# All 36 edge lookups of a pair in one block on TensorE, with three steps moved on VectorE

## The reference

```python
# graph layer, on layernorm(x)
ft = (feat @ W).reshape(n, H, OUT)                 # 4 heads of 64
e = e_src[src] + e_dst[dst]                        # per edge and head
e = where(e >= 0, e, 0.2 * e)
ex = exp(e - segment_max(e, dst)[dst])
a = ex / segment_sum(ex, dst)[dst] * dist
x = x + segment_sum(ft[src] * a, dst)
# experts, on layernorm(x): all eight for every node, weighted by a softmax over the experts
h = relu(bn1(x @ W1[e] + b1[e])); h = relu(bn2(h @ W2[e] + b2[e])); y = h @ Wo[e] + bo[e]
x = x + sum_e w[f, e] * y[f, e]
```

## Time and profile before

| | us |
|---|---|
| median of 3 runs | 1619.68 |
| lowest and highest | 1618.13, 1620.72 |
| the profiled execution | 1621.68 |
| its span, first to last instruction | 1620.1 |

### The profile page before, as it was taken

One profiled execution on the slowest core, in us unless ns is written; L12 is line 12 of the kernel. 1 busy time (PEld: TensorE's weight loads), 2 busy tenths in 40 slices (PEclk: granted clock), 3 DMA queues, 4 the chain that ended last, 5 costly groups with the idle time before them and its releaser, 6 DMA issues.

```text
span 1620.1 us, 23895 instructions
## 1 busy us (share of the span) xinstructions
PE 1492.8 (92%) x8358; PEld 1298.6 (80%) x8358; DVE 1184.3 (73%) x2195; ACT 749.2 (46%) x1341; POOL 1015.4 (63%) x934
## 2 busy tenths in 40 slices
PE   3670689999999999999999999999999999999998
PEld 2450577878888888888888888888888888888887
DVE  4660654578877887888788788878877887888751
ACT  1340133245555545545545555555455555545553
POOL 1027657767777777777777777777777777777000
PEclk9885799999999999999999999999999999999999
DMA  7765434434344434443443444343344434343000
GB/s 189 218 194 149 128 93 120 125 112 117 108 125 117 127 104 131 110 125 110 115 125 106 126 116 131 100 129 113 109 126 115 128 103 128 111 128 89 10 3 11
DMA packets 106161, 187.49 MB, mean 116 GB/s; under 512 B 38479, under 2 KB 70596, under 8 KB 106011
## 3 DMA queue, kind: packets, MB, share of 16 engines
q0 software_dynamic: 44144, 123.00, 27.6%
q1 hardware_dynamic: 61337, 62.42, 13.3%
q10 hardware_dynamic: 560, 0.52, 0.2%
HBM read 172.72 MB, written 14.42 MB: 116 GB/s over the span
## 4 chain that ended last, share of the span: by engine, by line
PE 70%; DVE 11%; issue 7%; ACT 4%; DMA 3%; SPq 3%; POOL 2%; ACTq 0%; DVEq 0%
PE bankH L786 35%; PE bankY L815 17%; PE bankE L745 5%; PE bankE L746 5%; PE bankE L738 3%; DMA table<-gath 3%; ACT msg_hi L967 3%; POOL gath L637 2%; DVE onehot L1345 2%; SPq L386 2%; PE bankB L723 1%; DVE x L1459 1%; DVE stats L1408 1%; DVE x L1406 1%; DVE x L1402 1%
## 5 line engine op out<-in xcount | busy, mean ns | idle before, releaser
L637 POOL DMA_INDIRECT gath<-table,src_win x900 | 1003.5, 1115 | 399.3 <-issue 224.6
L995 ACT ACTIVATE h<-bankH,bn_shift,bn_scale 128x250 f32<-128x250 f32 x800 | 401.7, 553 | 482.9 <-PE bankH L786 478.0
L786 PE MATMUL bankH<-h,w 128*128 128x250 f32 x1600 | 448.1, 399 | 0.0
L786 PE MATMUL bankH<-xT,w 128*128 128x250 f32 x1600 | 378.5, 379 | 1.6 <-ACT xT L981 1.4
L815 PE MATMUL bankY<-wo,h 128*125 128x256 f32 x1600 | 378.1, 379 | 1.1 <-DVE x L1459 1.1
L815 PEld LDWEIGHTS bankY<-wo,h 128*125 128x125 f32 x1600 | 296.2, 188 | 42.4 <-issue 1.4
L786 PEld LDWEIGHTS bankH<-xT,w 128*128 128x128 f32 x1600 | 296.9, 192 | 33.7 <-ACT xT L981 1.1
L1390 DVE TENSOR_TENSOR msg_lo<-gath,msg_hi 128x2340 fp32r<-128x2340 f32 x88 | 228.4, 2595 | 95.7 <-ACT msg_hi L967 95.7
L786 PEld LDWEIGHTS bankH<-h,w 128*128 128x128 f32 x1600 | 279.6, 199 | 18.1
L1459 DVE SCALAR_TENSOR_TENSOR x<-bankY,gate,x 125x256 f32<-125x256 f32 x400 | 174.0, 476 | 154.0 <-PE bankY L815 153.8
L967 ACT ACTIVATE msg_hi<-gath 128x2340 fp32r<-128x2340 f32 x88 | 189.2, 2150 | 190.7 <-PE bankE L746 190.7
(11 more groups left out here) (181 smaller groups left out, 972.9 us busy)
## 6 DMA issues: line engine op xcount, KB each, us to landing
onehot_t<-dst_low SPq DMA_DIRECT2D x48, 576.0 KB, 5.2
gath<-table,src_win POOLq DMA_INDIRECT x900, 2.8
x_res<-in_x SPq DMA_DIRECT2D x25, 250.0 KB
out<-x SPq DMA_DIRECT2D x25, 250.0 KB
table<-gath SPq DMA_DIRECT2D x25, 227.5 KB
w<-in_L_ffn_W SPq DMA_DIRECT2D x8, 512.0 KB, 5.5
wo<-in_L_ffn_Wo SPq DMA_DIRECT2D x4, 512.0 KB, 6.1
gath<-in_x SPq DMA_DIRECT2D x1, 2016.0 KB
```

What stands on the lines that cost most here:

```text
L637: pool.indirect_dma_start(gath[:, g.slot(u), t, :], None, table, bass.IndirectOffsetOnAxis(src_win[:, g.win, u, t:t + 1], 0)).then_inc(row ...
L786: mm = pe.matmul(target[:, hc * 2 * NT:(hc + 1) * 2 * NT], weights[:, e * KC + c, hc * P:(hc + 1) * P], operand(c), start=(c == 0), stop=( ...
L995: ins = act.activation(target[:, e % 2, hc, :, :].rearrange("p u n -> p (u n)"), source[:, hc * 2 * NT:(hc + 1) * 2 * NT], ACT.Relu, bias= ...
```

## The change

The 36 lookups of `a` are issued in one block, right behind `turn_bounds` in step `plan.bounds`; no `layer2` has lookups between its matmuls any more. On DVE, where `g` isn't late, `row_bounds(a)` goes from step 5 to the end of step 3, `runs(a)` comes ahead of `residual(g, 1)` in step 6, and `norm1(g, 0)` and `norm1(g, 1)` come behind that step's `add_y`. One row of the gathers is released in step 3 instead of step 4.

```diff
-BEHIND = (... (1, 1, 1, 2), (1, 2, 1, 2), ...)     # steps 3 and 4
+BEHIND = (... (1, 2, 1, 2), (1, 1, 1, 2), ...)
@@ PE, body
-                def between():
-                    for _ in range(2):
-                        next(small, None)
                     if a is not None and s == plan.bounds:
                         turn_bounds(f, a)
+                        for _ in small:
+                            pass
-                        layer2(*before(f, s, 1), between if 1 <= s <= 6 else nothing)
+                        layer2(*before(f, s, 1), nothing)
-                    if s == 6:
-                        for _ in small:
-                            pass
@@ DVE, body
-                    if a is not None and s == plan.bounds + 2:
+                    if a is not None and late(g) and s == plan.bounds + 2:
                         row_bounds(a)
                     ...
                             make_onehot(a, c)
+                    if a is not None and not late(a) and s == 6:
+                        runs(a)
                     if not late(g) and g is not None:
                         for u in plan.residuals.get(s, ()):
                             if u == 1:
                                 residual(g, u)
                     ...
-                    if a is not None and not late(a) and s == 6:
-                        runs(a)
-                    if f is not None and g is not None and not late(g) and s == max(plan.residuals):
-                        norm1(g, 0)
-                        norm1(g, 1)
                     if a is not None and not late(a) and s == 7:
                         edge_sum(a)
                         carries(a)
                     if run and (s >= 2 or not f.begins(1)):
                         add_y(*before(f, s, 2))
+                    if f is not None and g is not None and not late(g) and s == max(plan.residuals):
+                        norm1(g, 0)
+                        norm1(g, 1)
+                    if a is not None and not late(g) and s == plan.bounds:
+                        row_bounds(a)
```

More of the change, by code:

```diff
@@ L38 @@
 FROM = 5
-BEHIND = ((1, 1, 1, 0), (1, 1, 2, 0), (1, 1, 1, 2), (1, 1, 1, 2), (1, 2, 1, 2), (1, 1, 1, 2), (1, 1, 2, 0), (1, 1, 2, 0))
+BEHIND = ((1, 1, 1, 0), (1, 1, 2, 0), (1, 1, 1, 2), (1, 2, 1, 2), (1, 1, 1, 2), (1, 1, 1, 2), (1, 1, 2, 0), (1, 1, 2, 0))
 SEG = 2 * H
```

## The result

| | before | after |
|---|---|---|
| median of 20 runs each, us | 1620.57 | 1617.32 |
| lowest and highest | 1616.89, 1624.12 | 1613.13, 1619.19 |
| the profiled execution | 1621.68 | 1614.49 |
| its span | 1620.1 | 1612.9 |

The ratio is 0.9978, interval 0.9971 to 0.9985: the change makes the kernel faster by 0.22%, some 3.6 us. It was forecast to bring 9.1 us. The time is inside the range and the sign is right, but more than half of the forecast gain is missing.

A forecast was written before the change was run, and what follows sets the result against it. TensorE, busy 92% of the span, was taken to bound the kernel. Per steady body -1.04 + 1.76 - 0.33 - 0.33 - 0.49 = -0.43 us, -9.0 over 21, first two bodies -0.1: median 1610.6 us, range 1597 to 1619.

The forecast's parts named there:

- The price of the block: TensorE, step 3: 36 lookups in one group cost 2.28 us instead of 3.12 interleaved, saving 0.84 us a pair.
- The rival of lookups that are no cheaper: Block in step 3: each lookup costs 0.087 us, the block 3.12, body +0.41 us, kernel 1628; chance 6%.
- Steps 1 to 5: TensorE, steady body: steps 1 and 2 gain 1.04 us together, step 3 loses 1.76, steps 4 and 5 gain 0.33 each.
- Steps 6 and 7: Steady body: earlier start and no scans' wait, less a new `relu2` wait, bring 0.82 us, of which 0.49 is new.
- The wait for the scans: TensorE ahead of `turn_runs`, step 6: 0.61 us of waiting for VectorE's scans goes away with the reordering.
- The new wait for `relu2`: TensorE at `layer2` of expert 6, step 7: finds ScalarE's `relu2` unfinished and waits 0.65 us.
- the bodies of f = 0 and f = 1: First two full bodies: lookup savings -2.08 and -2.60 us, the block +2.28 in each, together -0.1 us.
- the fourth rival: TensorE's clock falls in the block: one layer a body at 1.2 GHz costs +1.68 us, kernel 1646; chance 2%.
- The sum: Whole kernel: -0.43 us per steady body, -9.0 over 21, first two bodies -0.1; median 1610.6 us.
- Without the `relu2` wait: Part of the rival that new waits don't come (18%): another 0.65 x 21 = 13.7 us saved, kernel 1597.
- Nothing holds TensorE inside the block for a one-hot: Answers the rival that release order makes TensorE wait inside the block for the second one-hot: 1619 us; chance 6%.
- The gathers are in time: Answers the rival that gathers come too late for `keep_esrc`: overrun by 0.4, the gain is gone, 1620 us; chance 8%.

The follow-up runs named there:

- r2_after: The changed kernel run once more with nothing altered, in a second set of runs: median 1615.84 us, ratio 0.9981 to the kernel before.
- e4_late_between: The changed kernel with the lookups of the bodies where `g` is late left between the matmuls of `layer2`: 1612.84 us, ratio 0.9958 to the kernel before.
- e5_relu2_late: `e4_late_between` with ScalarE's `relu2` of expert 5 ahead of both `root1` in step 6: 1600.96 us, ratio 0.9884 to the kernel before.
- e6_two_blocks: `e5_relu2_late` with the steady lookups in two blocks of 18, in steps 4 and 5: 1594.93 us, ratio 0.9850 to the kernel before.

## Why the prediction was right or wrong

- **The price of the block: right.** 2.21 us and 0.09 on the next layer (862.62 - 860.84 = 1.78 instead of 1.69), 2.30 in all; 2.28 was forecast. One lookup costs 0.061 us. The rival of lookups that are no cheaper (0.087) is out. The prediction's estimate by the Trainium skill, "TensorE: Matmul & The Clock Gate", section "Back-to-back issue gap", is out too: with its 81 ns a pair, given for 128 columns, 2.92 were to be expected, and for 12 columns this trace does not agree.
- **Steps 1 to 5: right.** -1.04 for steps 1 and 2 as forecast; +1.77 in step 3 (forecast +1.76); -0.36 each in steps 4 and 5 (forecast -0.33), where the loop from the chunk sum over `keep_high` and `low_part` takes 7.43 us (forecast 7.45).
- **Steps 6 and 7: the mechanism right, two sizes off.** Forecast -0.49, measured -0.34. The wait for the scans was taken as 2.14 - 1.53 = 0.61, the 1.53 from a `layer3` with a chunk sum behind it. With `turn_runs` behind it and no wait it takes 1.72, a case that the rows quoted did not hold. So only 0.42 of it was a wait; what follows a group changes the distance to the next start. The new wait for `relu2` was taken as 0.65 and is 0.57. The order of events was as forecast: 0.70 us of wait for `keep_esrc` (forecast 0.8), the scans, the second residual, `root1`, `relu2`. `norm1` behind `add_y` cost nothing, nor did `row_bounds` in step 3.
- **The step that failed: the bodies of f = 0 and f = 1, "together -0.1".** There the saving of each lookup was added up and the block's price set against it, with the price and the clock as in steady bodies. The medians say that they lose 3 to 4 us (the difference between the two groups of kernels). The traces say that it is two things: 2.7 us in the execution without a change of the clock, since savings ahead of a wait for VectorE only lengthen that wait and the block's own step costs more than in a steady body, and some 3 us more in the executions in which the clock falls behind the block. For the first, the forecast did not ask whether a saving in these bodies counts: TensorE waits there for the scans, 5.16 us at 215.06 in `r2_after` and 4.08 at 215.83 in `e4_late_between`, and that `turn_runs` starts 37.7 us behind the `turn_bounds` of the body before in both. For the second, the fourth rival, the clock falling in the block, was given 2% because the setup's block is at 1.00 after 2.07 us of idleness. In its form "one such layer a body" it is wrong. But the same row group that was quoted for it, an idle 3.85 us and a layer at half clock in the body of f = 1, said that just in these bodies the clock does fall.
- **The sum.** Terms as measured: 21 x -0.32 = -6.7 and +3.1 to +3.6 for the first bodies, against -9.0 and -0.1. The steady sizes explain 2.3 us of the miss, the first bodies 3.2 or more. That the time still fell inside the range says nothing for the term of the first bodies.
- **The other rivals.** Without the `relu2` wait the forecast gave 1597; that case is `e5_relu2_late`, and it took 1600.96, 3.96 over it. Its body is 0.90 us shorter than before, where -0.43 - 0.65 = -1.08 was forecast, and 21 x 0.18 = 3.8; the largest part is the 0.19 of the scans' wait that was none. Nothing holds TensorE inside the block for a one-hot: the next layer starts 2.20 us behind its start in the median of the steady bodies. The gathers are in time: L951 waits for them 4 times, the last time at 321.36 us, ahead of the steady bodies.
- **The whole block was worth less than its cover.** Of 0.84 us a pair, 0.16 in each of steps 4 and 5 becomes a wait for `msg_lo`; in step 6 the reordering is needed to pay it out; in step 7 0.57 go to `relu2`. `e6_two_blocks` shows the alternative: two blocks of 18 cost 1.08 us each plus 0.09 on the layer, where some 0.13 of each was a wait, and the body falls to 54.88.

Timeline of PE of `e6_two_blocks`, step 5:

```profile
805.60 1.85 PE L786 MATMUL bankH<-xT,w 128*128 128x250 f32 x8
807.29 1.23 PE L723 MATMUL bankB<-edst_parts,onehot_t 125*128 125x12 bf16 x18
808.37 1.94 PE L786 MATMUL bankH<-h,w 128*128 128x250 f32 x8
...
814.06 1.85 PE L786 MATMUL bankH<-xT,w 128*128 128x250 f32 x8
```

814.06 - 805.60 = 8.46 us, 1.04 over the 7.42 of after, where the block costs 1.17. It beats both kernels, by 1.5% and 1.3%.

## What to carry to other kernels

Work that is taken off the busiest engine in a step whose length is a loop between engines (chunk sum, `msg_hi`, `msg_lo`, chunk sum) turns into a wait there. Moved work is best put into just such steps: price each step by its own second-latest event, and then look at what is late next. A wait is the distance of starts less that of the same pair of groups without the wait; another successor gives another distance. Do the few bodies of the ramp with their own rows, above all where they have idle time on TensorE, and don't add up savings that stand ahead of a wait: two of them here took back about half of what 21 steady ones had brought.

## What the runs showed of the hardware

- **TensorE's clock behind a block of narrow matmuls.** 36 lookups of 12 columns at a granted clock of 1.00 were followed by 0.50, the level of 1.2 GHz, in the bodies of f = 0 and 1 of six executions out of seven. In the seven traces without a block there it stayed at 1.00. In the steady bodies it stayed at 1.00 throughout, with and without blocks, in all ten traces from chips without late signals. In the three executions with a fall on such chips TensorE had idled for 5.13 to 5.20 us some 15 us before the first block, and for 0.54 to 0.60 us right ahead of the second one; in the execution without a fall it was 5.13 and 0.61. What decides between them was not found: no run varied the idle time alone.
- **A chip on which signals come late.** On one chip the kernel before took 1664 us and after 1750. Steps with SyncE's two loads are those in which all engines of the core stand still for 2 to 6 us, until something that the profile names only as remote. Elsewhere these same loads, with DMA engines just as busy (99% and more), stop nothing. The losses grew with the change (1.0533 for after, 1.0090 for VectorE's order alone), so on that chip the change is a loss. The cause stays open; no run took a load away, and no trace of the kernel before was taken there.
- **Gathers under `low_part`.** GpSimd's gather takes 0.95 us, and the four of each body that meet VectorE's 2.60 us of `msg_lo` took 2.44 to 2.91 before. In after they take 2.90 to 3.38 in all but 2 of 83, since three of the four now start 0.05 to 0.25 us behind its start instead of 0.7 to 1.0; that is 2.2 us more a body (868.10 against 823.90 us over 20 bodies). In both kernels each such gather ends 0.82 or 0.83 us behind the end of `msg_lo`, so it is held until then. Under VectorE's `messages`, also a TENSOR_TENSOR and 2.55 us long, a gather takes 0.95 us as ever; what makes the difference was not tried. The hold cost nothing here, as GpSimd has time. Rows of after, VectorE and GpSimd:

```profile
803.49 2.60 DVE L1385 TENSOR_TENSOR msg_lo<-gath,msg_hi 128x2340 fp32r<-128x2340 f32 x1 [2.11 <-ACT msg_hi L962]
```
```profile
803.63 3.28 POOL L637 DMA_INDIRECT gath<-table,src_win  x1 [0.30 <-issue]
807.22 0.95 POOL L637 DMA_INDIRECT gath<-table,src_win  x1 [0.30 <-issue]
```
